# Moving the cross-attention folds from the routing stage into the first stage of a two-layer decoder kernel

## The reference

```python
# layer 0, block 2: a chain of quantised linears over the context
def bitnet_linear(x, W, b):
    w_scale = max(mean(abs(W)), 1e-5)
    qW = sign(W) * (abs(W) > 0.5 * w_scale)
    i_scale = max(max(abs(x)), 1e-8) / 127
    qx = clip(round(x / i_scale), -128, 127)
    return qx @ qW.T * (w_scale * i_scale) + b

vis = bitnet_linear(ctx, W_d2v, b_d2v)
image_embeds = bitnet_linear(vis, W_img, b_img)
kv_l = bitnet_linear(image_embeds, W_att_l, b_att_l)      # l = 0, 1

# layer 0, block 3: every token goes to one of 8 experts
top1 = argmax(softmax(x @ router_W + router_b))

# layer 1, block 2: cross attention, 16 heads of 64
q = xn @ Wq ; k, v = split(ctx @ Wkv)
out = softmax(q @ k.T / 8, masked) @ v @ Wo + bo
```

## Time and profile before

| | us |
|---|---|
| median of 3 runs | 1419.61 |
| lowest, highest | 1412.13, 1420.36 |
| the profiled execution | 1425.58 |
| its span, first to last instruction | 1423.6 |
| TensorE busy in the span | 1112.4 |
| VectorE busy in the span | 988.6 |

### The profile page before, as it was taken

One profiled execution on the slowest core, in us unless ns is written; L12 is line 12 of the kernel. 1 busy time (PEld: TensorE's weight loads), 2 busy tenths in 40 slices (PEclk: granted clock), 3 DMA queues, 4 the chain that ended last, 5 costly groups with the idle time before them and its releaser, 6 DMA issues. The chain is left out here.

```text
span 1423.6 us, 20621 instructions
## 1 busy us (share of the span) xinstructions
PE 1112.4 (78%) x6831; PEld 926.3 (65%) x6832; DVE 988.6 (69%) x1802; ACT 475.3 (33%) x1058; POOL 395.4 (28%) x541
## 2 busy tenths in 40 slices
PE   1488888667586879999822489898988999898987
PEld 0277777655165659888711268787777778687877
DVE  7699999555856102222249999999999999999610
ACT  0111111001063043232200155555555464555453
POOL 1112222100013400000040043625445353536353
PEclk9999999866778579999966789999999999999999
DMA  6035600000000836666353000000000000000000
GB/s 225 15 115 194 235 12 4 1 0 0 1 1 32 351 112 221 248 216 232 142 220 134 0 1 1 1 7 0 7 0 7 0 7 0 0 8 0 9 8 9
DMA packets 23972, 98.86 MB, mean 69 GB/s; under 512 B 3728, under 2 KB 15184, under 8 KB 17584
## 3 DMA queue, kind: packets, MB, share of 16 engines
q1 hardware_dynamic: 16080, 72.13, 13.5%
q10 hardware_dynamic: 5200, 18.85, 4.0%
q0 software_dynamic: 2640, 7.21, 1.5%
HBM read 87.96 MB, written 21.76 MB: 77 GB/s over the span
## 5 line engine op out<-in xcount | busy, mean ns | idle before, releaser
L1850 PE MATMUL bank<-n_hA_hi_reduced,ffn_h 128*128 128x256 f32 x512 | 129.2, 294 | 14.7 <-POOL n_hA_lo_reduced L1677 14.2
L1850 PE MATMUL bank<-n_hB_hi_reduced,ffn_h 128*128 128x256 f32 x512 | 125.8, 290 | 6.1 <-ACT n_hA_lo L1976 4.4
L1850 PE MATMUL bank<-n_hA_lo_reduced,ffn_h 128*128 128x256 f32 x512 | 125.5, 287 | 0.0
L1850 PE MATMUL bank<-n_hB_lo_reduced,ffn_h 128*128 128x256 f32 x512 | 120.3, 279 | 0.0
L1850 PEld LDWEIGHTS bank<-n_hA_hi_reduced,ffn_h 128*128 128x128 f32 x512 | 101.1, 197 | 18.4 <-POOL n_hA_lo_reduced L1677 17.0
L2088 DVE TENSOR_TENSOR d_prod<-d_qk,d_xT 128x512 f32<-128x512 f32 x128 | 104.5, 856 | 0.6
L1850 PEld LDWEIGHTS bank<-n_hB_hi_reduced,ffn_h 128*128 128x128 f32 x512 | 96.5, 189 | 9.4 <-ACT n_hA_lo L1976 5.8
L1850 PEld LDWEIGHTS bank<-n_hA_lo_reduced,ffn_h 128*128 128x128 f32 x512 | 101.3, 198 | 0.2
L1850 PEld LDWEIGHTS bank<-n_hB_lo_reduced,ffn_h 128*128 128x128 f32 x512 | 96.6, 189 | 1.8 <-issue 1.7
L1511 DVE TENSOR_TENSOR e_y<-bank,e_b 128x256 f32<-128x256 f32 x23 | 9.8, 424 | 124.0 <-PE bank L1441 124.0
L1486 ACT ACTIVATE e_hT<-bank,e_b 128x128 f32<-128x128 f32 x184 | 52.4, 368 | 127.2 <-PE bank L1429 127.2
(11 more groups left out here) (327 smaller groups left out, 2687.3 us busy)
## 6 DMA issues: line engine op xcount, KB each, us to landing
e_w<-in_W SPq DMA_DIRECT2D x23, 1024.0 KB
ffn_weights<-in_F ACTq DMA_DIRECT2D x2, 5632.0 KB, 20.0
e_piece<-ffn_weights SPq DMA_DIRECT2D x11, 1024.0 KB, 4.8
ffn_h<-ffn_weights SPq DMA_DIRECT2D x2, 4096.0 KB, 18.8
ffn_w<-ffn_weights SPq DMA_DIRECT2D x3, 1024.0 KB, 6.9
expert_rows<-zero ACTq DMA_DIRECT2D x1, 2944.0 KB, 11.6
e_xs<-expert_rows SPq DMA_DIRECT2D x23, 128.0 KB, 4.5
expert_out<-e_y POOLq DMA_DIRECT2D x23, 128.0 KB, 2.0
```

The costliest lines, as they stand in the source:

```text
L1850: last = nc.tensor.matmul(F[f % 2][:, 0:PAIR], weight(w[:, k, f * P:(f + 1) * P], fast), operand(src[part][1][:, k, :], fast), start=(c == ...
```

## The change

The folds leave `stage_route` and go to `stage_bits`, in pieces. On TensorE they stand between the chain's steps. Keys and values are cut by blocks: six blocks of keys in front of the d2v step; two of keys and two of values in front of the second turn; five of values in front of the img step; the last of values and one folded-queries piece in front of the third turn; one more in front of the att step; then the other two and the folded outputs of element 0, all in front of `summed(1)`. The folded outputs of element 1 come last. The copies go to ScalarE in `stage_bits`. `wkv` and `wqT` are asked for by SyncE in front of f1, the context (a second time, for the keys) and `wo1` by ScalarE. The loads leave `stage_attn0`. SyncE in routing no longer loads the context and no longer waits for the values before it asks for the first expert weights.

Three small results are also made that nothing reads yet: `q_txt_sum`, `b_txt_sum` and `cross01`, the last from two added matmuls.

```diff
@@ stage_bits, sync
             for n, (name, k, width, _) in enumerate(BITS):
+                if name == "f1":
+                    sp.dma_start(wkv[:, 0, :], ins["wkv"][0:P, :]).then_inc(wkv_loaded, 16)
+                    sp.dma_start(wkv[0:DC - P, 1, :], ins["wkv"][P:DC, :]).then_inc(wkv_loaded, 16)
+                    sp.dma_start(wqT[:, :, :], ins["wqT"]).then_inc(wqT_loaded, 16)
@@ stage_bits, scalar
             act.dma_start(m.bcol[:, :], ins["bcol"]).then_inc(small_loaded, 16)
+            act.dma_start(x_ctx[:, 0, :], ins["ctxT"][0:P, :]).then_inc(cxx_loaded, 16)
+            act.dma_start(x_ctx[0:DC - P, 1, :], ins["ctxT"][P:DC, :]).then_inc(cxx_loaded, 16)
...
             act.dma_start(m.sc1[:, :, :], ins["sc1"]).then_inc(small_loaded, 16)
+            act.dma_start(wo1[:, :, :], ins["wo1"]).then_inc(wo1_loaded, 16)
+            keys_or_values(0, KT)
+            keys_or_values(1, VT)
+            for b in range(B):
+                folded_queries(b)
+            for b in range(B):
+                folded_outputs(b)
@@ stage_bits, tensor
+            def keys_or_values(n, lo, hi):
+                if not n and not lo:
+                    pe.wait_ge(cxx_loaded, 32)
+                    pe.wait_ge(wkv_loaded, 32)
+                for f in range(lo, hi):
+                    c = f % 4 * P
+                    for k, rows in ((0, P), (1, DC - P)):
+                        last = nc.tensor.matmul(G[2 * n + f // 4][:, c:c + P],
+                                                wkv[0:rows, k, n * FF + f * P:n * FF + (f + 1) * P],
+                                                x_ctx[0:rows, k, :], start=(k == 0), stop=(k == 1))
+                if hi == KF:
+                    last.then_inc(kvx_done, 1)
...
             pe.wait_ge(consts_ready, 1)
             turned(0)
             summed(0)
+            keys_or_values(0, 0, 6)
             quantised(0, ("d2v",))
+            keys_or_values(0, 6, 8)
+            keys_or_values(1, 0, 2)
             turned(1)
+            keys_or_values(1, 2, 7)
             quantised(1, ("img",))
+            keys_or_values(1, 7, 8)
+            folded_queries(0, 0)
             turned(2)
+            folded_queries(0, 1)
             quantised(2, ("att0", "att1"))
+            folded_queries(1, 0)
+            folded_queries(1, 1)
+            pe.wait_ge(wo1_loaded, 16)
+            pe.wait_ge(small_loaded, 16 * 9)
+            folded_outputs(0)
             summed(1)
...
             last.then_inc(kv_turned, 1)
+            pe.wait_ge(mm_done, 3)
+            for b in range(B):
+                s = slice(b * SC, (b + 1) * SC)
+                last = nc.tensor.matmul(ps_b[0:SC, b * SC:(b + 1) * SC], m.kvT[:, 0, s], m.kvT[:, 1, s],
+                                        start=True, stop=True)
+            last.then_inc(products_done, 1)
+            folded_outputs(1)
@@ stage_bits, vector
             ternary("txt")
+            q_txt = m.q["txt"]
+            nc.vector.tensor_tensor(m.q_txt_sum[:, :, :], q_txt[:, :, 0:P], q_txt[:, :, P:2 * P], ALU.add)
+            nc.vector.tensor_tensor(m.b_txt_sum[:, :], m.bcol[:, 4:5], m.bcol[:, 5:6], ALU.add)
...
+            v.wait_ge(products_done, 1)
+            link(nc.vector.tensor_scalar(m.cross01[:, :, :].rearrange("p b s -> p (b s)"), ps_b[0:SC, 0:B * SC], 0.2, None,
+                                         ALU.mult))
@@ stage_attn0, scalar
             for i in range(-1, NT + 2):
-                if i == 2:
-                    later_weights()
-                elif i in (4, 6):
+                if i in (4, 6):
@@ stage_route, sync
-            for k, lo, n in ((0, 0, P), (1, P, DC - P)):
-                sp.dma_start(cx[0:n, k, :], ins["ctxT"][lo:lo + n, :]).then_inc(ctx_loaded, 16)
             sp.dma_start(m.w2e[:, :, :, :], ins["W2"]).then_inc(m.w2e_loaded, 16)
...
-            sp.wait_ge(kvx_done, 2)
             sp.wait_ge(slot_ready, 1)
@@ stage_route, tensor
-            pe.wait_ge(m.raws_loaded, 16 * 4)
-            pe.wait_ge(ctx_loaded, 32)
-            keys_or_values(0)
             pe.wait_ge(hot_ready, 1)
...
                 .then_inc(rank_done, 1)
-            keys_or_values(1)
-            for b in range(B):
-                folded_queries(b)
-            for b in range(B):
-                folded_outputs(b)
```

More of the change, by code:

```diff
@@ L160, in bits_map @@
     m.qx = s("qx", [P, KD, N], BF16)
+    m.q_txt_sum = s("q_txt_sum", [P, KD, P], BF16)
+    m.b_txt_sum = s("b_txt_sum", [P, 1], F32)
+    m.cross01 = s("cross01", [SC, B, SC], F32)
     m.work_a = s.at
@@ L1242, in folded_queries @@
-            def folded_queries(b):
-                for k in range(KD):
-                    n = b * KD + k
-                    if n >= 2:
-                        pe.wait_ge(fold_read, n - 1)
-                    else:
-                        pe.wait_ge(kvx_ready, n + 1)
-                    for h in range(H2):
-                        rows = slice(h % 2 * D2, (h % 2 + 1) * D2)
-                        last = nc.tensor.matmul(G[n % 2 * 2 + h % 2][:, h // 2 * SC:(h // 2 + 1) * SC],
-                                                m.wqT[rows, h // 2, k * P:(k + 1) * P],
-                                                KT[rows, h // 2, b * SC:(b + 1) * SC], start=True, stop=True)
-                    last.then_inc(fold_done, 1)
```

130 lines of the change are left out of this document (66 added, 64 removed).

## The result

| | us |
|---|---|
| before, median of 4 runs (lowest, highest) | 1418.9 (1412.1, 1420.4) |
| after, median of 4 runs (lowest, highest) | 1434.8 (1432.4, 1439.1) |
| ratio, with its 95% interval | 1.0125 (1.0084 to 1.0165) |
| the profiled execution of after, its span | 1439.1, 1437.4 |

The change costs 16 us, where "no change" was forecast at 1422 us; 1434.8 lies above the stated range of 1412 to 1430. Two later comparisons gave 1.0134 (1.0116 to 1.0152) and 1.0119 (1.0098 to 1.0140).

A forecast was written before the change was run, and what follows sets the result against it. Stages run between barriers; VectorE's chain fills the first, TensorE's folds and the ranking-and-scatter chain routing. First stage +31.9 and +0.3, routing -29.9, give +2.3 us on the profiled 1425.6, carried over to 1422 us; range 1412 to 1430.

The forecast's parts named there:

- What routing gives back: Routing without folds: first expert matmul at 494.5 us instead of 524.38, a gain of 29.9 us.
- the stretch: Routing, 489.3 to 500.6 us: TensorE had only 18 records in 11.3 us, which the prediction couldn't explain.
- the end of the shared transfers: Routing: 13.7 MB of weights, biases and rows at 0.42 MB/us take 32.6 us from 458.7, ending at 491.3.
- the third rival: Routing gives less because scatters, W2 and first weights share one stretch: -22 instead of -29.9, so 1430 us; chance 0.12.
- Behind the first expert matmul: The expert stage after its first matmul: the forecast sum has no term for it.
- What the first stage takes on: First stage with the folds: sums for f1 and f2 at 66.0 us instead of 34.1, so 31.9 us longer.
- The start of routing: Routing begins later by the first stage's +31.9 us and 0.3 us for `cross01`.
- The first: Rival: TensorE gets its high clock level in the first stage, whole kernel 23 us shorter, 1396 us; chance 0.08.
- The second rival: First stage: loads slow keys and values to 0.63 us a record, +17 us, so 1439 us; chance 0.12.
- the signs by which the prediction wanted to be found wrong: Key records at 0.12 or above 0.5 us, or routing not the scatters' 20 us plus 9.
- The sum: Whole kernel: +31.9 + 0.3 - 29.9 = +2.3 us on the profiled 1425.6, carried over to 1422 us.

The follow-up runs named there:

- i2: The kernel before, unchanged, profiled a second time: 1420.9 us in one execution, beside a median of 1416.5 us.
- j2: The kernel before with the first expert weights asked for behind the folded queries, not behind keys and values: 1417.4 us, ratio to before 0.9999.
- q: The kernel after, unchanged, compared once more with the kernel before: 1433.1 us, ratio 1.0119.
- k2: The kernel after with the lower 64 rows of the key and value weights laid on all 128 partitions: 1431.1 us, ratio to before 1.0107.
- d: The kernel after with the outputs' weights asked for by SyncE ahead of x, not early by ScalarE: 1434.95 us, ratio to before 1.0058.
- e: The kernel after, unchanged, run again beside the kernel before: 1435.3 us, ratio 1.0134.
- n: The kernel before, unchanged, profiled a third time: 1426.5 us, beside a median of 1427.0 us.
- f: The kernel after with all key and value matmuls over 128 rows, lower rows zero-filled: 1412.1 us, ratio to before 0.9970.
- h: The kernel before with rank matmuls first, keys and values over 128 rows, first expert weights asked for behind the folded queries: 1402.0 us, ratio 0.9902.
- g: The kernel after with all folds in one block behind the first stage's chain instead of in pieces: 1446.5 us, ratio to before 1.0209.
- o: The kernel before with the first expert weights asked for behind the folded queries, repeated on another chip: 1426.9 us, ratio 1.0002.
- m: The kernel before with rank matmuls ahead of the keys and all key and value matmuls over 128 rows, second run: 1413.9 us, ratio 0.9905.
- b: The kernel before with the two rank matmuls ahead of the keys, folds still in routing: 1419.2 us, ratio 0.9949.

## Why the prediction was wrong, by its own steps

**What routing gives back, -29.9: the step that failed.** It was the difference of 524.38 and an estimated 494.5. The first of these numbers holds 10 us that the typical execution doesn't have: the routing time of 66.7 us is one of a long chip, 56.9 that of a short one (i2, j2), and the timed runs of the kernel before (1412 to 1420) belong to the short kind, by their times (the record doesn't name the chips). The prediction saw the stretch, said that it couldn't explain it, and still counted its 10 us as given back. It even had the warning in its own base: the profiled execution was 6 us above the median of the runs, and this difference was carried over as if it were spread evenly over the kernel. Taking the stretch out of both numbers would have made the base 1415.6, the gain 19.9 and the forecast 1428.

The second number was too early by 3.3 us: the routing time of after is 40.1 us where the forecast had 36.8 (494.5 - 457.7). The rank matmuls, the chain to the slots and the end of the scatters came as worked out, at 9.56 and 29.8 us. The rows of the experts were asked for only at 36.75 us, and from there to the first matmul it took 3.35, as in the earlier trace rows. So the term that was too small is the end of the shared transfers: they moved at 371 GB/s over the 36.9 us of routing, where the forecast had put its 13.7 MB at 419. This is the third rival, at less than half of its price. (That rival's own sum has a slip: its 501.7 and the 3.3 us to the first matmul make 505.0 and -19.4, not 502.5 and -22.) Together: -29.9 + 10.0 + 3.3 = -16.6, and that is what q shows.

**Behind the first expert matmul: put at nothing.** In the nine profiles with folds and scatters in routing together, the second block of expert matmuls begins 7.8 to 8.5 us behind the first and the eighth 53.5 to 54.3. In the ten without folds there the numbers are 7.9 to 9.4 and 54.3 to 56.6; in five of these the second block also takes 5.1 to 5.4 us and not 3.74. So up to 2 or 3 us are lost where the forecast looked at nothing. The cause wasn't sought, and the total behind this point varies by 4 us between executions of one kernel, so it stands beside the sum and not in it.

**What the first stage takes on, +31.9: right.** The sums were read at 68.28, 65.73 and 65.98 in the three profiles of after, forecast 66.0. Two errors in it cancel. The key weights were not there at 17.4 but at 22.20, 19.64 and 20.64. From there to the sums it took 46.1 us (45.3 in q) and not the forecast's 48.6, since the steps partly overlap with the pieces (22.20 to 46.00 for keys, values and three steps, 1.1 us less than worked out; 46.00 to 61.02 for the queries and two steps, 0.6 less), and the outputs of the first element took 6.8 and not 7.5.

Of the late weights one cause is shown, the load on half of the partitions: k2 has its first key matmul at 17.10, below all five profiles with after's loads (18.32 to 22.20). Whether the outputs' weights beside them matter too, as d's 18.06 suggests, isn't shown. The forecast had used the 419 GB/s of the earlier trace rows, a stretch in which full-width loads ran, for a load that isn't one.

**The start of routing, +32.2: nearly right.** Measured were +35.5 in the given pair, and +33.2 and +33.5 for q and e against the 457.56 of n. `cross01` and what stands around it make 0.5 of the difference (13.8 us from the sums to the second stage, 82.05 - 68.28, and not 13.3, 47.42 - 34.16); about 1 us lies in the stages between, where executions of one kernel differ by as much, and was not followed up.

**The rivals.** The first (high level in the first stage, 1396) did not come for the kernel as it is, and for the reason given: mixed rows hold 0.363 us. f shows that it comes within the first keys when all of them have 128 rows (0.19 us, then 0.12). The Trainium skill (TensorE: Matmul & The Clock Gate, What's actually happening) says that activity lifts the engine to its upper level; the trace agrees for matmuls of 128 rows (granted 0.71, then 1.00 in h) and disagrees for those of 128 and 64 rows in turn (0.50 for 22.5 us in the earlier trace rows) and for those of 64 rows alone (0.50 for 13.6 us in i2). The second rival, keys slowed by the loads, is refuted as a mechanism: the pitch was 0.363 with the loads (after) and 0.365 without them (g). The time that it gave for the other side was near the truth, but by another mechanism, so its chance of 0.12 was not earned. Of the signs by which the prediction wanted to be found wrong, the keys' pitch gave none (0.363 us), but routing did: it took 36.75 us to the first load of the experts' rows, where "from some 490 to 522" had been said.

**The sum.** +31.9 + 0.3 - 29.9 = +2.3 was forecast; with the terms as measured it is +33.4 - 16.6 = +16.8. The three comparisons show +15.9, +18.8 and +16.3. On a long chip the change should cost some 10 us less: d, which differs from the kernel after in one load, is 8.4 us above before there.

Of the 48 us of folds that g has in one block, 33 showed in the kernel after; and of the same work on a short chip only 15.5 had shown in routing, where the scatters' 20 us and the transfers cover it. That is the main result: the folds left a stage where they were two thirds hidden for one where they are one third hidden.

## What to carry to other kernels

If a profiled execution is further from the median than the change is meant to bring, first find out which stretch makes the difference, and never credit a change with an unexplained stretch. Work that stands beside a long row of scatters is worth only what sticks out behind them; read that before moving it. The gain here lay in the form and order of the matmuls, in place: with all keys and values on 128 rows and the rank matmuls first, h gains 14.5 us. (It also asks late for the expert weights, which alone changed nothing in j2 and o.)

## What the runs showed of the hardware

- Float32 matmuls of 128 and 64 rows in turn take 0.363 us each; with the 64 rows filled up to 128 by zeros they take 0.134 us over all 64 (m) and 0.12 in a later piece (f), and the queries behind them 0.06 and not 0.11. It isn't enough that the heights are equal: the queries, 64 rows each, ran for 13.6 us at granted 0.50 (i2). What else decides it was not tried. k2, whose short matmuls of the values lie in partitions 64 to 127, has the same pitch as after.
- On two chips, and in the given profile, TensorE nearly stops for up to 16 us while GpSimd's scatters run (35 queries in 16.5 us, m), and runs freely 3.2 to 3.5 us behind the last scatter's issue. On two others (i2 and j2 on one, h on the other) queries beside scatters don't stop; for the fifth only the time of the kernel before, 1416.8 us, speaks. The cause is open. It begins at no fixed place: 6 us (m) or 21 us (b) behind the first scatter. The keys and values in b ran beside the scatters unharmed, 63 in 22.95 us.
- With a load into 64 partitions under way the DMA engines moved 155 to 209 GB/s at full DMA share (14 to 17 us, seven profiles), with the same bytes laid on all 128 partitions 433 (k2).
